# Rank-eight terms of two neighbouring output tiles as four 32-row matmuls in the array's four row strips

## The reference, cut to what matters

```python
h = tanh(concat(wte[idx], wte[idx shifted by 1], ..., by 15) @ w1 + b1)   # 64 wide
h = h @ w2 + b2                                                           # 1024 wide
h = h + autocorrelation_attention(layernorm(h))
n = layernorm(h)
h = h + (n @ W.T + bias + sum_e w_e (n @ A_e.T) @ Bf_e.T)
```

## Time and profile before

| | |
|---|---|
| median of 3 runs | 428.76 us (427.09 to 428.93) |
| span of the profiled execution | 440.3 us |
| instructions | 6477 |
| TensorE matmul busy | 409.3 us, 93% |
| DVE, ACT, GpSimd busy | 64%, 54%, 52% |
| written to HBM | 67.12 MB |

### The profile page before, as it was taken

The page is one execution under the profiler, slowest core; times in us unless marked ns, Lnnn a source line. Parts: engine busy times, 40 slices in busy tenths (PEclk is TensorE's granted clock), DMA queues, the critical chain, the costliest instruction groups (busy, mean ns, idle before and its releaser), DMA issues.

```text
span 440.3 us, 6477 instructions
## 1 busy us (share of the span) xinstructions
PE 409.3 (93%) x1886; PEld 318.6 (72%) x1886; DVE 282.6 (64%) x606; ACT 239.9 (54%) x359; POOL 229.5 (52%) x287
## 2 busy tenths in 40 slices
PE   2589969999999999999999999999999999999793
PEld 2465347888878777787878787878778878888582
DVE  3614866668585857677766758485857666775742
ACT  2215035666565656565656666565657556664632
POOL 6752383837566573737473847556465827131300
PEclk9999999999999999999999999999999999999998
DMA  5586002545545546354553544644636445454565
GB/s 99 186 266 255 1 16 67 218 143 222 185 192 208 199 154 247 116 223 176 189 210 125 228 165 194 211 191 172 233 110 263 145 190 209 163 218 175 207 253 228
DMA packets 27685, 79.86 MB, mean 181 GB/s; under 512 B 6187, under 2 KB 7483, under 8 KB 27669
## 3 DMA queue, kind: packets, MB, share of 16 engines
q1 hardware_dynamic: 23572, 75.46, 44.7%
q0 software_dynamic: 4096, 4.20, 4.9%
HBM read 12.40 MB, written 67.12 MB: 181 GB/s over the span
## 4 chain that ended last, share of the span: by engine, by line
PE 63%; POOL 13%; DVE 12%; issue 7%; ACT 2%; POOLq 1%; DMA 1%; another core or an unknown queue 1%; SPq 0%; DVEq 0%; ACTq 0%
PE o_ps L1064 35%; PE conv_ps L989 10%; PE conv_ps L992 5%; POOL beta L448 4%; POOL inv_std L438 4%; PE mix_ps L1096 2%; DVE u_rows L783 2%; DVE obuf L676 2%; PE sum_ps L1147 2%; PE sum_ps L1084 2%; DVE et_hl L754 2%; PE et_ps L1074 1%; DVE prod L773 1%; POOL var_eps L446 1%; POOL var_eps L436 1%
## 5 line engine op out<-in xcount | busy, mean ns | idle before, releaser
L500 ACT ACTIVATE obuf<-o_ps,mean_sb,a_sb 128x512 f32<-128x512 f32 x128 | 99.7, 779 | 98.4 <-PE o_ps L1064 83.4
L403 POOL DMA_INDIRECT gathered<-in_wte,idx_now x128 | 128.7, 1006 | 44.1 <-issue 34.9
L676 DVE TENSOR_SCALAR obuf<-o_ps,a_sb,mean_sb 128x512 f32<-128x512 f32 x128 | 102.6, 807 | 53.1 <-PE o_ps L1064 37.9
L1064 PE MATMUL o_ps<-w_hi,u_hi 128*128 128x512 f32 x256 | 104.8, 409 | 3.4 <-DVE obuf L676 2.5
L1064 PE MATMUL o_ps<-w_lo,u_hi 128*128 128x512 f32 x256 | 101.2, 395 | 0.0
L1064 PE MATMUL o_ps<-w_hi,u_lo 128*128 128x512 f32 x256 | 101.1, 395 | 0.0
L1064 PE MATMUL o_ps<-extra,xT 128*128 128x512 f32 x256 | 101.0, 394 | 0.0
L989 PE MATMUL conv_ps<-et_hl,shift_hi 128*128 128x512 f32 (+1 forms) x264 | 70.3, 409 | 5.1 <-DVE hT L764 2.8
L436 POOL TENSOR_SCALAR var_eps<-var 128x8 f32<-128x8 f32 x16 | 8.0, 501 | 110.1 <-DVE var L808 102.8
L989 PEld LDWEIGHTS conv_ps<-et_hl,shift_hi 128*128 128x128 f32 x264 | 50.2, 198 | 16.0 <-DVE hT L764 3.0
L1064 PEld LDWEIGHTS o_ps<-w_hi,u_hi 128*128 128x128 f32 x256 | 48.2, 188 | 17.8 <-issue 6.2
(11 more groups left out here) (133 smaller groups left out, 443.9 us busy)
## 6 DMA issues: line engine op xcount, KB each, us to landing
out<-obuf SPq DMA_DIRECT2D x63, 1024.0 KB, 4.0
h_all<-in_wT SPq DMA_DIRECT2D x4, 1024.0 KB, 9.9
gathered<-in_wte,idx_now POOLq DMA_INDIRECT x128
aT_sb<-in_aT SPq DMA_DIRECT2D x1, 1024.0 KB
bfT_sb<-in_bfT SPq DMA_DIRECT2D x1, 1024.0 KB, 13.6
obuf<-in_w SPq DMA_DIRECT2D x2, 256.0 KB
extra<-xbar_twice SPq DMA_DIRECT2D x1, 512.0 KB
out<-obuf SPq DMA_DIRECT2D x1, 512.0 KB
```

The source lines that it names most:

```text
L403: pool.indirect_dma_start(gathered[p][:, i, :], None, wte, bass.IndirectOffsetOnAxis(ap=idx_now[p][:, i:i + 1].bitcast(U32), axis=0),).the ...
L500: nc.scalar.activation(obuf[:, q, i % 2, 0:512], o_ps[:, 2 * (i % 2), :], ACT.Identity, bias=mean_sb[pc][:, i:i + 1], scale=a_sb[pc][:, i: ...
L676: nc.vector.tensor_scalar(obuf[:, q, i % 2, 512:L], o_ps[:, 2 * (i % 2) + 1, :], a_sb[pc][:, i:i + 1], mean_sb[pc][:, i:i + 1], ALU.mult, ...
L1064: last = mm(o_ps[:, 2 * (i % 2) + n, :], lhsT, rhs[:, 512 * n:512 * (n + 1)], start=(f == 0), stop=(f == len(factors) - 1))
```

## The change

The fourth matmul of each half tile, 128 rows of which eight hold data, goes. In its place the terms of two neighbouring tiles (four banks) are made by four matmuls of eight rows, at partitions 0, 32, 64 and 96 of `xT` and of one `extra[0]`, each into its own bank: banks 0 and 1 (even tile) end their sum with it, banks 2 and 3 (odd tile) begin theirs. `x_row` holds each tile's eight values twice, so `xT` has four blocks of 128 columns where it had two: TensorE makes four transposes of `x_row` where it made two, ACT copies 512 columns, and DVE's five steps on `x_row` write twice as much. TensorE's order is even tile (6 matmuls), four rank terms, odd tile (6 matmuls). Transposes, moments and conv halves keep their places between tiles; the four rank terms stand right behind the even tile and wait until the odd tile of the pair before (at the first pair, of the sequence before) was evicted. In step 2 the first of them wait for `rows_in`. The four memsets of `extra` on GpSimd and their semaphore go, with GpSimd's wait for `acf_done`, which SP takes; SP's three copies go into other rows of `extra[0]`.

```diff
@@ extra, xT, x_row
-        extra = [sb(f"extra{i}", [P, L], F32R) for i in range(4)]
+        extra = [sb(f"extra{i}", [P, L], F32R) for i in range(2)]
...
-        xT = [sb(f"xT{p}", [P, 2 * P], F32R) for p in range(2)]
+        xT = [sb(f"xT{p}", [P, NT // 2 * P], F32R) for p in range(2)]
...
-        x_row = sb("x_row", [P, NT, XW], F32R)
+        x_row = sb("x_row", [P, NT, 2, XW], F32R)
@@ SP
-            sp.wait_ge(extra_zeroed, 1)
+            sp.wait_ge(acf_done, 1)
...
             for i in range(1, 4):
-                sp.dma_start(extra[i][XW * i:XW * i + NX, :].bitcast(F32), extra[0][0:NX, :].bitcast(F32)).then_inc(rows_in, 16)
+                sp.dma_start(extra[0][XW * i:XW * i + NX, :].bitcast(F32), extra[0][0:NX, :].bitcast(F32)).then_inc(rows_in, 16)
@@ GpSimd
-                if in_step(1, g, u):
-                    pool.wait_ge(acf_done, 1)
-                    for i in range(4):
-                        last_fill = pool.memset(extra[i][:, :].bitcast(F32), 0.0)
-                    last_fill.then_inc(extra_zeroed, 1)
@@ ACT
-                    nc.scalar.copy(xT[pb][:, :], et_ps[:, 0:2 * P]).then_inc(xt_kept, 1)
+                    nc.scalar.copy(xT[pb][:, :], et_ps[:, :]).then_inc(xt_kept, 1)
@@ DVE, scale_h
-                    nc.vector.tensor_copy(x_row[:, :, 2:4], beta[:, :].unsqueeze(2).to_broadcast([P, NT, 2])).then_inc(x_step, 1)
+                    nc.vector.tensor_copy(x_row[:, :, :, 2:4], both(beta).unsqueeze(3).to_broadcast([P, NT, 2, 2])).then_inc(x_step, 1)
...
@@ TensorE
-                def tile_product(i):
...
-                    factors = ((u_hi[u][:, cols], w_hi), (u_lo[u][:, cols], w_hi), (u_hi[u][:, cols], w_lo),
-                               (xT[u][:, P * (i // 4):P * (i // 4 + 1)], extra[i % 4]))
...
+                def main_products(i):
+
+                    cols = slice(P * i, P * (i + 1))
+                    factors = ((u_hi[u][:, cols], w_hi), (u_lo[u][:, cols], w_hi), (u_hi[u][:, cols], w_lo))
+                    for n in range(2):
+                        for f, (lhsT, rhs) in enumerate(factors):
+                            last = mm(o_ps[:, 2 * (i % 2) + n, :], lhsT, rhs[:, 512 * n:512 * (n + 1)],
+                                      start=(i % 2 == 0 and f == 0), stop=(i % 2 == 1 and f == len(factors) - 1))
+                    return last
...
+                    ge(pe, oa_kept, NT * c + 2 * q - 1)
+                    ge(pe, ov_kept, NT * c + 2 * q - 1)
+                    main_products(2 * q)
+
+                def four_rank_terms(q):
+
+                    if q == 0 and in_step(2, g, u):
                         pe.wait_ge(rows_in, 48)
 
+                    ge(pe, oa_kept, NT * c + 2 * q)
+                    ge(pe, ov_kept, NT * c + 2 * q)
+                    for k in range(4):
+                        rows = slice(XW * k, XW * k + NX)
+                        ins = mm(o_ps[:, k, :], xT[u][rows, P * q:P * (q + 1)], extra[0][rows, 512 * (k % 2):512 * (k % 2 + 1)],
+                                 start=(k >= 2), stop=(k < 2))
+                        if k == 1:
+                            ins.then_inc(o_done, 1)
+
+                def odd_tile(q):
+
+                    main_products(2 * q + 1).then_inc(o_done, 1)
@@ TensorE, order of the step
-                    tile_product(0)
+                    even_tile(0)
+                    four_rank_terms(0)
...
-                    tile_product(1)
+                    odd_tile(0)
...
-                    tile_product(2)
-                if back:
-                    tile_product(3)
+                    even_tile(1)
+                    four_rank_terms(1)
+                    odd_tile(1)
...
-                    tile_product(4)
-                    tile_product(5)
+                    even_tile(2)
+                    four_rank_terms(2)
+                    odd_tile(2)
                 if back and not front:
-                    tile_product(6)
+                    even_tile(3)
+                    four_rank_terms(3)
...
-                    for hh in range(2):
-                        last = tr(et_ps[:, P * hh:P * (hh + 1)],
-                                  x_row[:, 4 * hh:4 * hh + 4, :].bitcast(F32).rearrange("p i x -> p (i x)"), ident_sb[:, :])
+                    for q in range(NT // 2):
+                        last = tr(et_ps[:, P * q:P * (q + 1)],
+                                  x_row[:, 2 * q:2 * q + 2, :, :].bitcast(F32).rearrange("p i d x -> p (i d x)"), ident_sb[:, :])
...
                 if back and front:
-                    tile_product(6)
-                if back:
-                    tile_product(7)
+                    even_tile(3)
+                    four_rank_terms(3)
+                if back:
+                    odd_tile(3)
```

More of the change, by code:

```diff
@@ L228, in tower_kernel @@
         w_hi_set = sem("w_hi_set")
-        extra_zeroed = sem("extra_zeroed")
         w_set = sem("w_set")
@@ L411, in _ @@
                 gather_rows(0, i)
-            pool.memset(x_row[:, :, :].bitcast(F32), 0.0)
+            pool.memset(x_row[:, :, :, :].bitcast(F32), 0.0)
             pool.memset(minus_half[:, :], -0.5)
@@ L417, in _ @@
             pool.wait_ge(zeros_set, 1)
-            pool.memset(x_row[:, :, 0:2].bitcast(F32), 1.0).then_inc(zeros_set, 1)
+            pool.memset(x_row[:, :, :, 0:2].bitcast(F32), 1.0).then_inc(zeros_set, 1)
             def step(g, u, front, mid, back, last=False):
@@ L778, in variance, with both @@
                     nc.vector.tensor_reduce(in_pairs(quad[:, :])[:, pairs], products, AX.X, ALU.add).then_inc(quad_ready, 1)
+                def both(col):
+                    return col[:, :].unsqueeze(2).to_broadcast([P, NT, 2])
                 def scale_h():
@@ L785, in scale_h @@
                     nc.vector.reciprocal(inv_a[:, :], a_sb[pb][:, :]).then_inc(x_step, 1)
-                    nc.vector.tensor_copy(x_row[:, :, 2:4], beta[:, :].unsqueeze(2).to_broadcast([P, NT, 2])).then_inc(x_step, 1)
+                    nc.vector.tensor_copy(x_row[:, :, :, 2:4], both(beta).unsqueeze(3).to_broadcast([P, NT, 2, 2])).then_inc(x_step, 1)
                     dve.wait_ge(x_step, 3 * b + 1)
-                    nc.vector.tensor_copy(x_row[:, :, 5:7], inv_a[:, :].unsqueeze(2).to_broadcast([P, NT, 2])).then_inc(x_step, 1)
+                    nc.vector.tensor_copy(x_row[:, :, :, 5:7], both(inv_a).unsqueeze(3).to_broadcast([P, NT, 2, 2])).then_inc(x_step, 1)
                     dve.wait_ge(x_step, 3 * b + 2)
-                    nc.vector.tensor_tensor(x_row[:, :, 4], beta[:, :], x_row[:, :, 2].bitcast(F32), ALU.subtract)
+                    nc.vector.tensor_tensor(x_row[:, :, :, 4], both(beta), x_row[:, :, :, 2].bitcast(F32), ALU.subtract)
                     dve.wait_ge(x_step, 3 * b + 3)
-                    nc.vector.tensor_tensor(x_row[:, :, 7], inv_a[:, :], x_row[:, :, 5].bitcast(F32),
+                    nc.vector.tensor_tensor(x_row[:, :, :, 7], both(inv_a), x_row[:, :, :, 5].bitcast(F32),
                                             ALU.subtract).then_inc(x_ready, 1)
@@ L1044, in step, with even_tile @@
                 pb = 1 - u
-                def tile_product(i):
-                    if i == 0:
+                def main_products(i):
[6 more added lines that the diff above has]
+                    return last
+                def even_tile(q):
+                    if q == 0:
                         pe.wait_ge(h_hi_kept, c + 1)
```

9 lines of the change are left out of this document (removed).

## The result

| | before | after |
|---|---|---|
| median of runs | 427.92 us (426.44 to 428.93) | 423.67 us (423.29 to 423.80) |
| ratio | | 0.988 [0.9835, 0.9925] |
| span of a profiled execution | 440.3, a second one 427.0 | 421.4 us |

In four later sets of runs, each on a chip of its own, the kernel before had medians of 429.3 to 431.0 us; in the one with 431.01 the changed kernel ran beside it, with 423.54 and a ratio of 0.983 [0.980, 0.985]. Two executions of those sets, 516.67 us of e12 and 817.17 us of the kernel before, are left out of every ratio.

What follows compares the result with a forecast made beforehand. TensorE was taken to bound stretch A and a DVE/GpSimd chain stretch B. Gains of 2.8 (A), 1.2 (B), 3.1 (start) and 1.4 (end) sum to 8.5 us off the median 428.76: forecast 420 us, range 413 to 434.

Steps and rivals of the forecast that it cites:

- The forecast case: Four strips load and stream side by side, p from 0.30 to 0.65: 414.5 to 425.5 us; chance 0.44.
- p: TensorE time of one pack of four 32-row matmuls, put at 0.233 + 2 x 0.09 + 3 x 0.025 = 0.48 us.
- Its own formula: The total time changes by 32 us for each us of p: 28 packs in Stretch A, 4 at the end.
- stretch B: Transposes of h to those of beta*h, 14.46 us: DVE/GpSimd chain binds; nothing won in nine long periods, 1.2 us in five others.
- The rival without overlap: In each pack no strip overlaps, four matmuls take turns: p = 1.11, 443 us, slower; chance 0.14.
- the one of loads in line: In each pack weight loads go in line, streams together: p = 0.73, 428 us, no change; chance 0.17.
- so a change from a wide to a one-row matmul costs 0.09: Price of each array-shape switch around a pack, read from L983 and L984 at the start: 0.52 - 0.43 us.
- The draining rival: The array empties at each shape switch around a pack: p = 0.80, 430.5 us; chance 0.13.
- Stretch A: Transposes of beta*h to those of h, 9.27 us: only TensorE sets the time; 0.20 won each, 2.8 us in 14.
- The start: Without GpSimd's memsets of extra, conv half 1 starts at 60.4 instead of 63.49: 3.1 us, bounds 0.7 and 3.6.
- this load is hidden, beta comes before DVE asks for it: GpSimd's 7.32 us idle before L436, read as a code load, moves ahead of its input; DVE's 4.57 us wait goes.
- The end: Last sequence's tiles alone save 1.8; a wait for tile 5's eviction in the step before costs about 0.4: together 1.4 us.

Runs made afterwards that it cites:

- e12: Kernel before (128-row products) with early GpSimd memsets, tile 0 behind the transposes of h, DVE's scaling ahead of tile 4's eviction: 430.95 us, ratio 1.0025.
- e3: Changed kernel with each pack's four matmuls issued twice, evicting engines of the even tile told only after all eight: 435.23 us.
- e4: Changed kernel with only two of each pack's four matmuls, those of banks 1 and 2: 423.25 us.
- e0: Kernel before, unchanged, run again for a second profile: 429.15 us, span 427.0.
- e2: Changed kernel with GpSimd's four memsets put back on scratch tiles, behind their old wait for acf_done: 425.61 us, ratio 0.9894.
- e8: Changed kernel itself, unaltered, run again on the chip of its variants: 423.54 us, ratio 0.9827 to the kernel before.
- e9: Changed kernel with tile 0 moved behind the transposes of h and DVE's scaling ahead of its eviction of tile 4: 414.76 us, ratio 0.9674.
- e5: Changed kernel with four 128-row matmuls in each pack's place, on tiles zeroed early: 434.81 us, ratio 1.0101 to the kernel before.
- e10: Changed kernel with only DVE's scaling of h put ahead of its eviction of tile 4: 424.18 us.

## Why the prediction was right or wrong

- **The case and its size.** Faster was forecast, with 420 us; it is 423.67, inside the range, and the gain is about half of the 8.5 forecast (4.3 between medians, 5.6 between the ordinary spans). The forecast case (p up to 0.65) is the one that came, at its upper end. Its own formula with the measured p gives 8.5 - 32 x 0.15 = 3.7, near the measured gain. That is partly luck, since errors in stretch B, at the start and at the end went both ways.
- **The strips overlap** (right). The rival without overlap fell with the four starts within 0.02, the one of loads in line with e3 and e4.
- **The size of p** (wrong, 0.63 for 0.48). The step that failed is "so a change from a wide to a one-row matmul costs 0.09", taken twice. It was read from two matmuls of one column and three, at the start; between streams of 512 columns e3 and e4 give 0.40 for two changes. The pack's first matmul shows 0.09, the return to wide ones 0.20 and then another 0.10. The draining rival expected such a fixed cost, at a higher price (p = 0.80); whether the array really empties no run shows. The Trainium skill (TensorEngine Tiling, Key Properties) states that a change of tiling mode drains TensorE; e3 and e4 agree in that the cost hangs on the change alone, not on how many matmuls lie between. The other term, 3 x 0.025 for issuing, should go: e4 saves nothing with two fewer.
- **Stretch A** (its sum right, its p wrong). The working with the measured p gives 9.06 - 1.40 + 1.26 + 0.24 = 9.16; measured are 9.19 to 9.28. The term of 0.05 for the longer steps on `x_row` was too small: in the ten looped periods the transposes of `x_row` come 0.63 behind those of beta*h, 0.43 in e0. Instead of 2.8 us gained, 14 times 0.13 to 0.21 was lost.
- **Stretch B** (the chain right, its share wrong). "Stretch B pays almost nothing" rested on nine long periods that an ordinary execution does not have. With the measured p, TensorE's work there is 13.91 - 2.33 + 1.26 = 12.84. In the ten periods of GpSimd's loop L1167 waits 0.5 for the chain, and pack 1 starts 0.1 or 0.2 late behind tile 1's eviction, and B ends at 13.64 to 13.76, a gain of 0.15 to 0.27, near the 0.25 that was put down for short periods. In the four others GpSimd's chain is shorter and B is 13.07 to 13.19, a gain of 0.7 to 0.9. The prediction's sign, TensorE waiting about a microsecond or more in every period, failed: it is 0.5 in ten. Stretches A and B together give 2.5 us where 4.0 were forecast.
- **The start** (3.1 forecast, 3.06 measured: the number by luck). Conv half 1 was to start 3.1 earlier. It starts at 56.75 where e0 has 58.58, 1.83 earlier. The 3.1 was read from the longer profile, in which DVE waits 4.57 for beta; in e0 it waits 3.32. Another 1.46 comes from TensorE's clock, which the prediction did not have. In e0 TensorE stood still for 2.60, and while it then worked at conv half 1 the granted clock was 0.62; in the changed kernel the wait is 0.52 and the clock 1.00. Windows of conv half 1, e0 and the changed kernel:

```profile
58.58:63.04 4.46, 4.46 (x13) 3.53 (x14) 2.57 (x3) 2.24 (x4) 3.52 (x5) 0.62 0.19 32
56.75:59.75 3.00, 3.00 (x12) 2.21 (x13) 2.57 (x3) 2.46 (x4) 2.42 (x4) 1.00 0.19 36
```

  Tile 0 and its pack give 0.23 back. The step that failed is "this load is hidden, beta comes before DVE asks for it": L430 began 1.34 after its input, the steps behind it were slow (under e2), and DVE still waited 1.57 for beta. The inference that a load of about 6 us would be over in time falls with it: GpSimd had nothing to do for 12.01 us ahead of L430 and was late all the same. Nor does any run show that the idling is a load of code. What was right is the place: with beta earlier, conv half 1 waits for ACT's copy (DVE's L758 waited 0.93 for it). Pack 0 of step 2 waited 0.54 for the rows of `extra`, 1.7 in e8; the prediction had put this copy 0.7 ahead of its need, and it was not.
- **The end** (1.4 forecast, 0.07 and, in e8, 1.3 measured). From the last L1167 to the end it takes 24.65 instead of 25.57, a gain of 0.9 out of the 1.8 forecast: four packs cost 0.15 more each, and the two more transposes of `x_row` some 0.2, which the sum left out here. The last stretch B took 15.22 instead of 14.37. e8 had 14.00, so the forecast loss of 0.4 in that stretch is not a fixed one.
- **The base.** The sum was taken off a span of 440.3 and the difference carried to the median. The terms of an execution that is 11.5 us above the median were those of an execution of another shape; those of an ordinary one would have shown TensorE, not the chain, as the bound in stretch B, and a shorter wait at the start.

## What to carry to other kernels

A pack of row strips costs one stream plus 0.40 us for the two changes of shape here, however many matmuls it holds: put as much work of the narrow shape as possible between two changes, and count p from start to start beyond the neighbours' pace, over two matmuls behind the pack. After matmuls are taken away, look at which chain runs beside them; here most of the gain (9.4 of the 15.0 us between the spans of before and e9) waited in a chain and behind evictions until the order was changed, and the order alone, without the strips, was worth nothing or less. A wait taken off TensorE can bring its clock back as well: split such a gain into the earlier start and the faster matmuls behind it. Before reading slack from a profile, compare its span with the runs' times, and read one of an ordinary execution.

## What the runs showed of the hardware

**The cost of changing shape comes in three places:** 0.09 before the pack, 0.20 at the first wide matmul after it and 0.10 at the second; the last two are outside the pack's own records, so that the mean duration of the group (0.498 against 0.394) doesn't show them.

**A wait of TensorE was followed by the lower clock in some profiles and not in others.** In the last stretch B the changed kernel waits for DVE's eviction of tile 4. Timeline of TensorE in its first profile:

```profile
390.92 0.39 PE L1050 MATMUL o_ps<-w_lo,u_hi 128*128 128x512 f32 x1
393.19 0.72 PE L1050 MATMUL o_ps<-w_hi,u_hi 128*128 128x512 f32 x1 [1.88 <-DVE obuf L670]
393.70 0.63 PE L1050 MATMUL o_ps<-w_hi,u_lo 128*128 128x512 f32 x1
394.13 0.63 PE L1050 MATMUL o_ps<-w_lo,u_hi 128*128 128x512 f32 x1
```

and its window, with a mean granted clock of 0.72:

```profile
391.00:397.00 6.00, 4.12 (x15) 2.39 (x14) 3.99 (x11) 1.18 (x3) 0.65 (x2) 0.72 0.41 164
```

The matmuls come 0.43 apart there (1.2 GHz) instead of 0.233. In e8 the same wait of 1.9 left the clock at 1.00, and the stretch was 1.2 shorter. At the start it is the other way round: in e8 pack 0 of step 2 waited 1.66 and the granted clock was 0.65 from 62.37 to 65.00, which made the first steady period 23.74; the first profile had a wait of 0.54 there, a clock of 1.00 and 22.27. Behind waits of 1.62 in e5 and 2.70 in e9 the matmuls kept their pace of 0.233; behind 3.03 in e10 they came 0.43 apart. So the length of the wait alone does not decide it. The runs of e9 at 414.3 to 414.9 us have a mean granted clock of 0.995, its two at 417.0 of 0.985 and 0.991; whether this clock step is the cause was not tried.

**The idling after the memsets** was 6.64, 7.32 and 7.38 us in three profiles (e0, e2), and the input was there when it began. In the eleven profiles with the memsets early or gone, GpSimd's first step still began 0.3 (e10) to 3.5 us (e12) after its input, and the seven steps took 7.5 to 9.5 us instead of 5.6 to 6.2.
